# The softmax maxima of a cross-attention kernel are split and turned on VectorE

## The chip, the cores and the metric

The kernel runs on one core of one Trainium2 chip. The metric is device time in microseconds (us), the median of the runs; lower is better. The core has TensorE (PE, its weight loads are listed as PEld), VectorE (DVE), ScalarE (ACT), GpSimd (POOL) and the queues that issue DMAs (SP among them). They run beside each other, each in the order of its own program, and wait for each other by semaphores.

## The reference

Cross-attention with pre-norm on both inputs, 32 batches of 512 tokens, width 512, 16 heads of 32:

```python
B, N_q, _ = q.shape                       # 32, 512, 512; kv has the same shape
qn  = layer_norm(q,  q_norm_g,  q_norm_b)
kvn = layer_norm(kv, kv_norm_g, kv_norm_b)
Q = (qn @ Wq), K = (kvn @ Wk), V = (kvn @ Wv)      # each cut into 16 heads of 32
scores = einsum('bhqd,bhkd->bhqk', Q, K) / sqrt(32)
attn = softmax(scores, axis=-1)
ctx  = einsum('bhqk,bhkd->bhqd', attn, V)
out  = q + gelu(ctx @ Wo + bo, approximate=False)
```

All of it is float32. The softmax needs, for each query and head, a shift by the largest score of its row.

## The kernel before

**Tiling.** A batch is worked off in four steps (s = 0 to 3). A step takes one unit: four heads (128 columns of Q and K). What stands in a step belongs to several units and batches at once: the scores `s` (queries in the partitions, only for the maxima) of the unit one ahead, the scores `st` (keys in the partitions), exponentials and products `pv` with V of the unit itself, the projections `q` and `k` of the unit two ahead, the row sums `z` of the unit behind; and over the batch the projections `v`, the output projections `o` (of the batch before) and the transposes `x` of the tokens (of the batch after).

**The order is written out by hand.** `ORDER` (from line 51) lists for each engine and step the kinds in the order in which the engine takes them; `s*4` is four times `s`. PE takes a projection (12 matmuls of 512 columns) in six parts of two, woven between the scores. An engine never overtakes itself.

**How the maxima get into the scores.** In a step DVE reduces 16 `s` tiles, each to 128 negated maxima (L706), one column of `maxes` each: column 4n+c holds the maxima of head n for the c-th chunk of 128 queries. The shift is then added by TensorE itself: of the 128 rows that `st` contracts, rows 96 to 127 hold the maxima (`q_stack`) against a mask of heads (`k_stack`). For this the maxima have to lie in 32 rows, queries along the free axis, and as a high part rounded to the matmul's input format (16 rows) and the rest (16 rows), so that nothing of them is lost. That goes over five instructions:

1. `md`, DVE L765: copies the 16 columns beside themselves (a maximum over groups of one).
2. `m`, PE L965: one 128x128 transpose of `maxes` into a PSUM bank of the `gen` ring.
3. `mh`, ACT L613: rounds (and for the low rows negates) 32x128 into `max_cut`.
4. `ml`, DVE L771: adds for the low rows the unrounded value, into `max_hl`.
5. `mx`, ACT L617, four times: writes 32x512 of `q_stack`, masked by chunk (a column of `chunk_mask`). The first `st` of the next step waits for all four (`shift_rows`).

**PSUM.** Four banks hold scores (a bank is free when its exponential, L563, or maximum, L706, has been taken), one holds `ctx`, and three (`gen0` to `gen2`) go round among everything in `GEN`: q, k, v, o, x, z and m. Which bank comes next, and whose release it waits for, follows from the order on PE alone.

**Output side.** The output projection of a chunk is followed on DVE by `ob` (L747, adds the bias in the bank), on ACT by `gelu` (L580, into `act_out`, with a table load before the first and one before the next exponential, L563), and on POOL by `res_add`. Of the four chunks of a batch, the `ob` and `gelu` of the third stand at the end of step 1, around `md`, `mh` and `mx`; the fourth stands in step 2.

Of the kernel before, what the change touches and what calls it, by code (L numbers as in the profile page):

```python
# [12 lines left out]
P = 128  # L13
# [47 lines left out]
    ),  # L61
    "act": (
# [4 lines left out]
    ),  # L67
    "dve": (
# [93 lines left out]
for _s in range(NU):  # L162
    for _kind, _n, _part in PLAN["pe"][_s]:
# [3 lines left out]
        if _part == 0 and _kind in ("q", "k", "m", "z"):  # L167
            _off = _s + {"q": 2, "k": 2, "m": 1, "z": -1}[_kind]
            GEN_AT[(_kind, _off % NU)] = len(GEN)
            GEN.append((_kind, _off // NU, _off % NU, NU))  # L170
# [8 lines left out]
def build(nc, x, ctx_in, q_g, q_b, kv_g, kv_b, wq, wk, wv, wo, bo, out):  # L179
    B = x.shape[0]  # L180
    with ExitStack() as es:
# [6 lines left out]
        def sem(name):  # L188
            return es.enter_context(nc.semaphore(name))
# [19 lines left out]
        maxes = sb("maxes", [P, 2, P])  # L209
        max_cut = sb("max_cut", [P, P], F32R)  # L210
        max_hl = sb("max_hl", [P, P], F32R)
        cut_sign = sb("cut_sign", [P, 1])
        low_row = sb("low_row", [P, 1])
# [20 lines left out]
        full = {k: sem(f"{k}_in_psum") for k in "vomzxqk"}  # L234
        free = {k: sem(f"{k}_out_of_psum") for k in "vomzxqk"}
# [8 lines left out]
        max_cut_done = sem("max_cut_done")  # L244
        max_copied = sem("max_copied")
# [191 lines left out]
        def _(pool):  # L437
# [3 lines left out]
            pool.memset(low_row[:], 0.0).then_inc(consts, 1)  # L441
            pool.memset(cut_sign[:], 1.0).then_inc(consts, 1)
            pool.memset(act_out[:], 0.0).then_inc(act_out_free, 1)
            pool.wait_ge(consts, 5)
            pool.affine_select(out=ident[:], in_=ident[:], compare_op=ALU.not_equal, fill=1.0, base=0,
                               pattern=[[-1, P]], channel_multiplier=1).then_inc(consts, 1)
            pool.wait_ge(consts, 6)
            pool.affine_select(out=cut_sign[:], in_=cut_sign[:], compare_op=ALU.is_ge, fill=-1.0,
                               base=SROW + SHIFTS // 2 - 1, pattern=[[0, 1]], channel_multiplier=-1).then_inc(consts, 1)
            pool.wait_ge(consts, 7)  # L450
            pool.affine_select(out=low_row[:], in_=low_row[:], compare_op=ALU.is_ge, fill=1.0,
                               base=SROW + SHIFTS // 2 - 1, pattern=[[0, 1]], channel_multiplier=-1).then_inc(consts, 1)
# [56 lines left out]
        def _(act):  # L509
# [36 lines left out]
            def batch(b):  # L546
                PLAN = plan_of(b)
                for s in range(NU):
# [4 lines left out]
                    for kind, n, part in PLAN["act"][s]:  # L553
# [71 lines left out]
        def _(dve):  # L625
            dve.memset(maxes[:], 0.0)
# [64 lines left out]
            def batch(b):  # L691
                PLAN = plan_of(b)
                for s in range(NU):
# [298 lines left out]
```

## Time and profile before

| | |
|---|---|
| median of 3 runs | 3264.93 us (3263.69 to 3266.2) |
| the profiled execution | 3262.8 us, of it 3261.0 us from first to last instruction |
| PE busy | 3230.8 us (99%), 16611 matmuls |
| DVE, ACT, POOL busy | 2256.9 us (69%), 2280.3 us (70%), 2313.9 us (71%) |
| TensorE's granted clock | 0.998 of full speed |
| one batch | about 99.7 us, nearly the same for batches 1 to 30 |

Matmuls overlap in the profile (a matmul of 512 columns is listed with 0.39 to 0.41 us, and the next one starts 0.23 us after it), so what a PE instruction costs is read from the starts of its neighbours. In a timeline the columns are: start in us, length in us, engine, line, operation, tiles, shapes, count; in brackets the idle time of the engine before it and what ended it. A row of several instructions (x4) gives the time from the first start to the last end.

### The profile page before, as it was taken

To read this page: it belongs to the slowest core of one execution; us is meant where nothing else is said; L and a number is where in the kernel's file an instruction comes from. 1 tells how busy PE (TensorE), PEld (TensorE's weight loads), DVE (VectorE), ACT (ScalarE), POOL (GpSimd) and SP (SyncE) were. 2 spreads that over 40 slices of the span, in tenths; PEclk is the share of its full clock that TensorE was granted. 3 is DMA by queue.
4 is the path that set the end of the run, shared out by engine and by line. 5 is a ranking of instruction groups with operands and counts; after the bars stand their busy time and mean duration, and the time that the engine had idled before them with its cause. 6 is when DMAs were issued, how large, how long until landed. Compare 5 with 4: busy or idle time off the path is not lost.

```text
span 3261.0 us, 49855 instructions
## 1 busy us (share of the span) xinstructions
PE 3230.8 (99%) x16611; PEld 2135.1 (65%) x16611; DVE 2256.9 (69%) x4769; ACT 2280.3 (70%) x3985; POOL 2313.9 (71%) x1544
## 2 busy tenths in 40 slices
PE   8999999999999999999999999999999999999998
PEld 5566666666666666666666666666666666666664
DVE  6667667676676676666766766766667767667664
ACT  5677666777767777667767667776777676677765
POOL 3676776777677767777776677777767776777765
PEclk9999999999999999999999999999999999999999
DMA  5655656566556656565665566665656655666653
GB/s 142 87 108 107 108 104 116 91 111 107 107 104 104 111 107 107 104 118 89 111 109 106 105 102 111 109 104 104 120 86 112 107 107 107 100 111 108 105 79 76
DMA packets 186721, 343.02 MB, mean 105 GB/s; under 512 B 20561, under 2 KB 20577, under 8 KB 186466
## 3 DMA queue, kind: packets, MB, share of 16 engines
q1 hardware_dynamic: 186000, 339.03, 60.0%
q8 instruction: 134, 2.20, 0.3%
q10 hardware_dynamic: 466, 0.80, 0.2%
q14 instruction: 121, 0.99, 0.1%
HBM read 104.87 MB, written 33.55 MB: 42 GB/s over the span
## 4 chain that ended last, share of the span: by engine, by line
PE 97%; DVE 1%; ACT 1%; issue 1%; DMA 0%; POOL 0%; SPq 0%; ACTq 0%; POOLq 0%; DVEq 0%
PE gen L856 43%; PE score L883 16%; PE score L876 15%; PE ctx L903 14%; PE gen L847 4%; PE gen L943 4%; PE gen L965 1%; DVE maxes L706 1%; DMA k_stack<-k_nat 0%; ACT q_stack L617 0%; PE score L788 0%; ACT probs L563 0%; DVE stats L725 0%; PE gen L837 0%; POOL probs L475 0%
## 5 line engine op out<-in xcount | busy, mean ns | idle before, releaser
L475 POOL TENSOR_TENSOR probs<-probs 128x1024 f32<-128x1024 f32 x762 | 1800.3, 2392 | 287.8 <-PE ctx L903 281.6
L706 DVE TENSOR_REDUCE maxes<-score 128x1 f32<-128x512 f32 x2048 | 1294.9, 680 | 217.5 <-PE score L883 213.9
L563 ACT ACTIVATE probs<-score 128x512 f32<-128x512 f32 x2048 | 1090.2, 621 | 141.1 <-PE score L876 137.5
L883 PE MATMUL score<-k_stack,q_stack 96*128 96x512 f32 x2048 | 761.2, 413 | 3.3 <-DVE maxes L706 1.8
L876 PE MATMUL score<-q_stack,k_stack 128*128 128x512 f32 x2048 | 696.4, 406 | 6.6 <-ACT q_stack L617 6.5
L883 PEld LDWEIGHTS score<-k_stack,q_stack 96*128 96x128 f32 x2048 | 378.2, 188 | 221.3 <-ACT probs L563 83.6
L876 PEld LDWEIGHTS score<-q_stack,k_stack 128*128 128x128 f32 x2048 | 374.7, 188 | 199.9 <-DVE maxes L706 64.4
L903 PE MATMUL ctx<-probs,v_sb 128*32 128x512 f32 x4096 | 492.5, 598 | 0.0
L856 PE MATMUL gen<-cT,w_k 128*128 128x512 f32 x1536 | 461.7, 400 | 0.2 <-DVE q_nat L688 0.2
L856 PE MATMUL gen<-w_v,cT 128*128 128x512 f32 x1536 | 461.4, 395 | 0.0
L856 PE MATMUL gen<-xT,w_q 128*128 128x512 f32 x1536 | 447.9, 394 | 0.0
L856 PE MATMUL gen<-w_o,ctx_hl 128*128 128x512 f32 x1488 | 416.4, 396 | 0.0
L491 POOL TENSOR_TENSOR rstd<-var_eps,minus_half 128x1 f32<-128x1 f32 x256 | 140.5, 549 | 335.0 <-DVE neg_mean L737 333.1
L502 POOL TENSOR_TENSOR ctx_hl<-ctx_n,ctx_hl 128x512 fp32r<-128x512 f32 x128 | 164.2, 1283 | 290.4 <-ACT ctx_hl L569 290.4
L617 ACT ACTIVATE q_stack<-max_hl,chunk_mask 32x512 fp32r<-32x512 f32 x512 | 326.3, 706 | 42.3 <-DVE max_hl L771 41.5
L856 PEld LDWEIGHTS gen<-w_v,cT 128*128 128x128 f32 x1536 | 287.3, 189 | 84.1 <-issue 26.8
L856 PEld LDWEIGHTS gen<-xT,w_q 128*128 128x128 f32 x1536 | 288.5, 190 | 60.6
L856 PEld LDWEIGHTS gen<-cT,w_k 128*128 128x128 f32 x1536 | 287.5, 192 | 55.2 <-DVE q_nat L688 1.1
L688 DVE SCALAR_TENSOR_TENSOR k_nat<-gen,bias_k,k_nat 128x512 fp32r<-128x512 f32 x128 | 95.8, 748 | 318.0 <-ACT k_nat L608 318.0
L856 PEld LDWEIGHTS gen<-w_o,ctx_hl 128*128 128x128 f32 x1488 | 276.7, 189 | 57.3
L903 PEld LDWEIGHTS ctx<-probs,v_sb 128*32 128x32 f32 x4096 | 106.9, 109 | 233.8 <-issue 233.8
L574 ACT ACTIVATE v_sb<-gen 128x512 f32<-128x512 f32 x128 | 76.5, 598 | 255.1 <-PE gen L856 255.1
(89 smaller groups left out, 2765.4 us busy)
## 6 DMA issues: line engine op xcount, KB each, us to landing
k_stack<-k_nat SPq DMA_DIRECT2D x384, 256.0 KB, 7.6
q_stack<-q_nat SPq DMA_DIRECT2D x381, 256.0 KB, 5.6
tok<-in_x SPq DMA_DIRECT2D x132, 256.0 KB, 11.0
tok<-in_ctx SPq DMA_DIRECT2D x128, 256.0 KB, 12.0
res<-in_x SPq DMA_DIRECT2D x124, 256.0 KB, 2.7
out<-res SPq DMA_DIRECT2D x124, 256.0 KB, 2.1
probs<-in_L_xattn_Wq SPq DMA_DIRECT2D x1, 1024.0 KB, 8.2
probs<-in_L_xattn_Wk SPq DMA_DIRECT2D x1, 1024.0 KB, 10.4
```

What stands on the lines that cost most here:

```text
L475: pool.tensor_tensor(probs[:, c + 1, heads], probs[:, c + 1, heads], probs[:, c, heads], ALU.add).then_inc(pool_added, 1)
L491: pool.tensor_tensor(rstd[:, n:n + 1], var_eps[:, n:n + 1], minus_half[:], ALU.pow).then_inc(ln_rstd, 1)
L502: pool.tensor_tensor(ctx_hl[:, 1, up], ctx_n[:], raw(ctx_hl[:, 0, up]), ALU.subtract).then_inc(ctx_split, 1)
L563: act.activation(probs[:, n, part, :], score_at(s, "st", i)[:], ACT.Exp, scale=SCALE).then_inc(exp_done, 1)
L617: act.activation(q_stack[SROW:P, u1 % 2, :, P * n:P * (n + 1)], raw(max_hl[SROW:P, :]).unsqueeze(1).to_broadcast([SHIFTS, HU, P]), ACT.Ide ...
L706: dve.tensor_reduce(maxes[:, u1 % 2, SROW + i:SROW + i + 1], score_at(s, "s", i)[:], AX_X, ALU.max, negate=True).then_inc(max_done, 1)
L847: mm = pe.matmul(bank[DH * j:DH * (j + 1), :], ones[:, 0:DH], probs[:, c, j, :], start=(i == 0), stop=(i == len(chunks) - 1))
L856: mm = pe.matmul(bank[:, :], stationary(hs, c), moving(hm, c), start=(i == 0), stop=(i == len(TERMS) * NC - 1))
L876: pe.matmul(score_bank(pe, b, s, "st", i)[:, :], k_stack[:, s % 2, part, P * n:P * (n + 1)], q_stack[:, s % 2, part, :], start=True, stop= ...
L883: pe.matmul(score_bank(pe, b, s, "s", i)[:, :], q_stack[0:KROWS, u1 % 2, n, P * part:P * (part + 1)], k_stack[0:KROWS, u1 % 2, n, :], star ...
L903: mm = pe.matmul(ctx_ps[DH * j:DH * (j + 1), :], v_sb[:, c, lo:lo + DH], probs[:, c, j, :], start=(c == 0), stop=(c == NC - 1))
L943: mm = pe.matmul(bank[:, P * c:P * (c + 1)], tok[:, n, P * c:P * (c + 1)], ident[:], start=True, stop=True, is_transpose=True)
```

## The change

The transpose on PE and the rounding on ACT go; DVE does both. `md` keeps its place in DVE's order and now stands for six instructions:

- a reduction over groups of one writes the 16 columns rounded into `max_split[:, 0:16]`;
- `scalar_tensor_tensor` writes `maxes * 1 - rounded` into `max_split[:, 16:32]`; it waits for the first by a semaphore;
- four `transpose` of 32x32 turn partitions 32g to 32g+31 of `max_split` into rows 96 to 127 of `max_hl`, columns 32g to 32g+31; the first waits for the subtraction.

`mh`, `m` and `ml` leave the orders, which otherwise stay as they are; `mx` waits for the four transposes. `m` also leaves the ring of `gen` banks. Two memsets and two selects at the start of the program go.

```diff
@@ ORDER
     "pe": (
-        "st s k s*2 pv m k o*2 k o k*2",
+        "st s k s*2 pv k o*2 k o k*2",
...
     "act": (
...
-        "st*6 gelu q st x st*2 norm st*4 x k st*2 norm x norm st x*2 norm x norm x*2 gelu mh gelu mx*4 split",
+        "st*6 gelu q st x st*2 norm st*4 x k st*2 norm x norm st x*2 norm x norm x*2 gelu gelu mx*4 split",
...
     "dve": (
...
-        "ln la*2 q zt lv*2 x la zr ln zb cn lv s la x k lv s x s*2 x*2 s*2 x s*3 x s*2 x s ob s*4 md ob ml",
-        "s ob s*6 zt s zr zb cn s k s*7 md q ml",
+        "ln la*2 q zt lv*2 x la zr ln zb cn lv s la x k lv s x s*2 x*2 s*2 x s*3 x s*2 x s ob s*4 md ob",
+        "s ob s*6 zt s zr zb cn s k s*7 md q",
@@ GEN
-        if _part == 0 and _kind in ("q", "k", "m", "z"):
+        if _part == 0 and _kind in ("q", "k", "z"):
@@ scalar engine
-                        if kind == "mh" and valid(b1):
-                            wait(act, full["m"], NU * b1 + u1 + 1)
-                            wait(act, free["m"], NU * b1 + u1)
-                            act.activation(max_cut[SROW:P, :], gen_at("m", u1)[SROW:P, 0:P], ACT.Identity,
-                                           scale=cut_sign[SROW:P, 0:1]).then_inc(max_cut_done, 1)
                         if kind == "mx" and valid(b1):
-                            wait(act, free["m"], NU * b1 + u1 + 1)
+                            wait(act, max_turned, HU * (NU * b1 + u1 + 1))
@@ vector engine
                         if kind == "md" and valid(b1):
                             wait(dve, max_done, 16 * (t1 + 1))
-                            dve.tensor_reduce(maxes[:, u1 % 2, SROW + SHIFTS // 2:P],
-                                              maxes[:, u1 % 2, SROW:SROW + SHIFTS // 2].unsqueeze(2), AX_X,
-                                              ALU.max).then_inc(max_copied, 1)
-                        if kind == "ml" and valid(b1):
-                            wait(dve, max_cut_done, t1 + 1)
+                            dve.tensor_reduce(max_split[:, 0:SHIFTS // 2], maxes[:].unsqueeze(2), AX_X,
+                                              ALU.max).then_inc(max_high, 1)
+                            wait(dve, max_high, t1 + 1)
+                            dve.scalar_tensor_tensor(out=max_split[:, SHIFTS // 2:SHIFTS], in0=maxes[:], scalar=ones[:, 0:1],
+                                                     in1=raw(max_split[:, 0:SHIFTS // 2]), op0=ALU.mult,
+                                                     op1=ALU.subtract).then_inc(max_low, 1)
                             wait(dve, shift_rows, NC * t1)
-                            dve.scalar_tensor_tensor(out=max_hl[SROW:P, :], in0=gen_at("m", u1)[SROW:P, 0:P],
-                                                     scalar=low_row[SROW:P, 0:1], in1=raw(max_cut[SROW:P, :]),
-                                                     op0=ALU.mult, op1=ALU.add).then_inc(free["m"], 1)
+                            wait(dve, max_low, t1 + 1)
+                            for g in range(P // SHIFTS):
+                                rows = slice(SHIFTS * g, SHIFTS * (g + 1))
+                                dve.transpose(max_hl[SROW:P, rows], raw(max_split[rows, :])).then_inc(max_turned, 1)
@@ tensor engine
-                        if kind == "m" and valid(b1):
-                            bank = gen_bank(pe, b, "m", u1)
-                            wait(pe, max_copied, t1 + 1)
-                            pe.matmul(bank[:, 0:P],
-                                      maxes[:, u1 % 2, :], ident[:], start=True, stop=True,
-                                      is_transpose=True).then_inc(full["m"], 1)
```

How the rows of the program stand, in a batch in the middle. DVE at the end of step 1, before: L706 is the maximum of a score tile, L765 `md`, L747 `ob`, L771 `ml`.

```order
L706 TENSOR_REDUCE maxes<-score3 128x1 [waits s_full]
L765 TENSOR_REDUCE maxes<-maxes 128x16 [waits max_done]
L747 TENSOR_TENSOR gen1<-gen1,bias_all 128x512 [waits o_in_psum]
L771 SCALAR_TENSOR_TENSOR max_hl<-gen0,low_row,max_cut 32x128 [waits shift_rows,max_cut_done]
L706 TENSOR_REDUCE maxes<-score0 128x1 [waits s_full,m_in_psum]
L747 TENSOR_TENSOR gen2<-gen2,bias_all 128x512 [waits o_in_psum]
```

The same place in the changed kernel: L689 is the maximum of a score tile, L730 `ob`.

```order
L689 TENSOR_REDUCE maxes<-score3 128x1 [waits s_full]
L748 TENSOR_REDUCE max_split<-maxes 128x16 [waits max_done]
L751 SCALAR_TENSOR_TENSOR max_split<-maxes,ones,max_split 128x16 [waits max_high]
L758 STREAM_TRANSPOSE max_hl<-max_split 32x32 [waits max_low,shift_rows]
L758 STREAM_TRANSPOSE max_hl<-max_split 32x32 x3
L730 TENSOR_TENSOR gen0<-gen0,bias_all 128x512 [waits o_in_psum]
L689 TENSOR_REDUCE maxes<-score0 128x1 [waits s_full]
```

Before, one instruction stood between the last maximum and `ob`; now six do.

ACT at the same place, before and then after: L580 and L571 are `gelu`, L617 and L603 `mx`, L569 and L560 the split of `ctx`, L563 and L554 the exponentials.

```order
L580 ACTIVATE act_out<-gen2 128x512 [waits o_biased]
L613 ACTIVATE max_cut<-gen0,cut_sign 32x128 [waits m_out_of_psum,m_in_psum]
L580 ACTIVATE act_out<-gen1 128x512 [waits act_out_free,o_biased]
L617 ACTIVATE q_stack<-max_hl,chunk_mask 32x4x128 [waits m_out_of_psum] x4
L569 ACTIVATE ctx_hl<-ctx_n 128x512 [waits o_in_psum,ctx_read]
L580 ACTIVATE act_out<-gen2 128x512 [waits act_out_free,o_biased]
L563 ACT_TABLE_LOAD [waits st_full]
L563 ACTIVATE probs<-score0 128x512 [waits pool_added]
```

```order
L571 ACTIVATE act_out<-gen1 128x512 [waits o_biased]
L571 ACTIVATE act_out<-gen0 128x512 [waits act_out_free,o_biased]
L603 ACTIVATE q_stack<-max_hl,chunk_mask 32x4x128 [waits max_turned] x4
L560 ACTIVATE ctx_hl<-ctx_n 128x512 [waits o_in_psum,ctx_read]
L571 ACTIVATE act_out<-gen1 128x512 [waits act_out_free,o_biased]
L554 ACT_TABLE_LOAD [waits st_full]
L554 ACTIVATE probs<-score0 128x512 [waits pool_added]
```

The rounding is gone from between the two gelus; the second gelu still stands ahead of `mx` and still waits for its `ob`.

PE at the end of step 2, before and then after: L903 and L888 are `pv`, L965 is `m`, L856 and L841 are projections.

```order
L903 MATMUL ctx<-probs,v_sb 32x512 x7
L965 MATMUL gen1<-ident,maxes 128x128 [waits max_copied,k_out_of_psum]
L856 MATMUL gen2<-cT,w_k 128x512 [waits z_out_of_psum]
L856 MATMUL gen2<-cT,w_k 128x512
L856 MATMUL gen0<-xT,w_q 128x512 [waits q_out_of_psum]
L856 MATMUL gen0<-xT,w_q 128x512
L856 MATMUL gen2<-cT,w_k 128x512 x2
L856 MATMUL gen1<-w_v,cT 128x512 [waits x_out_of_psum,m_out_of_psum]
```

```order
L888 MATMUL ctx<-probs,v_sb 32x512 x7
L841 MATMUL gen2<-cT,w_k 128x512 [waits k_out_of_psum]
L841 MATMUL gen2<-cT,w_k 128x512
L841 MATMUL gen0<-xT,w_q 128x512 [waits z_out_of_psum]
L841 MATMUL gen0<-xT,w_q 128x512
L841 MATMUL gen2<-cT,w_k 128x512 x2
L841 MATMUL gen1<-w_v,cT 128x512 [waits x_out_of_psum,q_out_of_psum]
```

The transpose is gone, and the first matmul of `v` waits for the bank of the `q` of the step before (released by DVE's L673, the L688 of before) where it waited for the bank of `m`.

## Rows read from the trace of the kernel before

**Rows 1.** The page: busy times, and the chain that ended last.
```profile
PE 3230.8 (99%) x16611; PEld 2135.1 (65%) x16611; DVE 2256.9 (69%) x4769; ACT 2280.3 (70%) x3985; POOL 2313.9 (71%) x1544
PE 97%; DVE 1%; ACT 1%; issue 1%; DMA 0%; POOL 0%; SPq 0%; ACTq 0%; POOLq 0%; DVEq 0%
```

**Rows 2.** Timeline of PE, seam of steps 1 and 2.
```profile
1011.90 0.30 PE L965 MATMUL gen<-ident,maxes 128*128 128x128 f32 x1
1011.95 2.07 PE L856 MATMUL gen<-w_o,ctx_hl 128*128 128x512 f32 x8
1013.86 0.40 PE L883 MATMUL score<-k_stack,q_stack 96*128 96x512 f32 x1
...
1016.20 0.40 PE L876 MATMUL score<-q_stack,k_stack 128*128 128x512 f32 x1
```

**Rows 3.** Timeline of PE, a `pv` without and one with `m` behind.
```profile
1027.20 0.73 PE L883 MATMUL score<-k_stack,q_stack 96*128 96x512 f32 x2
1027.76 0.40 PE L856 MATMUL gen<-xT,w_q 128*128 128x512 f32 x1
...
1032.75 0.33 PE L965 MATMUL gen<-ident,maxes 128*128 128x128 f32 x1
1032.83 0.71 PE L856 MATMUL gen<-cT,w_k 128*128 128x512 f32 x2
1033.38 0.62 PE L856 MATMUL gen<-xT,w_q 128*128 128x512 f32 x2
```

**Rows 4.** Timeline of DVE, seam of steps 1 and 2.
```profile
1009.07 2.47 DVE L706 TENSOR_REDUCE maxes<-score 128x1 f32<-128x512 f32 x4
1011.58 0.17 DVE L765 TENSOR_REDUCE maxes<-maxes 128x16 f32<-128x16 f32 x1
1011.67 0.69 DVE L747 TENSOR_TENSOR gen<-gen,bias_all 128x512 f32<-128x512 f32 x1
1012.63 0.36 DVE L771 SCALAR_TENSOR_TENSOR max_hl<-gen,low_row,max_cut 32x128 fp32r<-32x128 f32 x1 [0.27 <-ACT max_cut L613]
```

**Rows 5.** Timeline of ACT, the same seam.
```profile
1012.24 0.36 ACT L613 ACTIVATE max_cut<-gen,cut_sign 32x128 fp32r<-32x128 f32 x1 [2.44 <-PE gen L965]
1012.62 0.60 ACT L580 ACTIVATE act_out<-gen 128x512 f32<-128x512 f32 x1
1013.24 2.55 ACT L617 ACTIVATE q_stack<-max_hl,chunk_mask 32x512 fp32r<-32x512 f32 x4
...
1016.35 0.58 ACT L580 ACTIVATE act_out<-gen 128x512 f32<-128x512 f32 x1
1016.95 1.28 ACT L563 ACT_TABLE_LOAD   x1
1018.25 2.06 ACT L563 ACTIVATE probs<-score 128x512 f32<-128x512 f32 x4
```

**Rows 6.** Timeline of PE's weight loads, step 2 and the start of step 3.
```profile
1018.90 0.19 PEld L883 LDWEIGHTS score<-k_stack,q_stack 96*128 96x128 f32 x1 [0.26 <-ACT probs L563]
...
1034.07 0.41 PEld L856 LDWEIGHTS gen<-w_v,cT 128*128 128x128 f32 x2
...
1036.51 0.30 PEld L876 LDWEIGHTS score<-q_stack,k_stack 128*128 128x128 f32 x2 [0.21 <-ACT q_stack L617]
```

**Rows 7.** Groups of instructions on DVE (count | busy us, mean ns | idle before).
```profile
L688 DVE SCALAR_TENSOR_TENSOR q_nat<-gen,bias_q,q_nat 128x512 fp32r<-128x512 f32 x128 | 95.5, 746 | 222.5 <-ACT q_nat L594 222.5
L711 DVE STREAM_TRANSPOSE ctx_n<-gen 128x512 f32<-128x512 f32 x128 | 90.3, 705 | 62.4 <-PE gen L847 62.4
```

**Rows 8.** Timeline of DVE, seams of steps 2 and 3, and of 0 and 1.
```profile
1032.04 0.17 DVE L765 TENSOR_REDUCE maxes<-maxes 128x16 f32<-128x16 f32 x1
...
1078.80 0.17 DVE L765 TENSOR_REDUCE maxes<-maxes 128x16 f32<-128x16 f32 x1
1080.20 0.36 DVE L771 SCALAR_TENSOR_TENSOR max_hl<-gen,low_row,max_cut 32x128 fp32r<-32x128 f32 x1 [1.23 <-ACT max_cut L613]
1080.59 0.69 DVE L725 BATCH_NORM_STATS2 stats<-tok 128x6 f32<-128x512 f32 x1
```

More of the change, by code:

```diff
@@ L53 @@
         "q*3 v q*2 v q v st*2 v*2 s st v s st s v*2 st s st s z v st*3 s v*2 st*2 s st k v s*4 pv st s st*2 o s "
[1 row of a table removed]
[1 row of a table added]
         "o st*2 o st*3 q st q*4 st q st*3 z x k*3 x st*2 x st k*2 s k st s st*2 pv s x s x s x s pv s x s*2 o*3 "
[1 row of a table removed]
[1 row of a table added]
         "o*4 s o s k s k s st k s st z st s st s q st q st s st*2 k st*3 k s st k st*4 pv s*2 q s q s*2 q s*2 q "
[1 row of a table removed]
[1 row of a table added]
         "k q k v q v k*2 st*3 k st*2 q st*2 k q st q st q st*2 z st*4 v st v s*3 pv s*2 v s*2 v s*2 v s v s*2 v*2 "
[1 row of a table removed]
[1 row of a table added]
     ),
     "act": (
[4 rows of a table removed]
+        "q st*4 v st*8 norm v split norm*2 st*4 mx*4 k",
+        "st*6 gelu q st x st*2 norm st*4 x k st*2 norm x norm st x*2 norm x norm x*2 gelu gelu mx*4 split",
+        "gelu st*12 k split st*4 q mx*4",
+        "st*6 k st*5 q st*4 split st v*2 mx*4",
     ),
     "dve": (
[4 rows of a table removed]
[4 rows of a table added]
     ),
@@ L208, in build @@
         ones = sb("ones", [P, P])
[L209 to L213, printed above, removed]
+        maxes = sb("maxes", [P, SHIFTS // 2])
+        max_split = sb("max_split", [P, SHIFTS], F32R)
+        max_hl = sb("max_hl", [P, P])
         chunk_mask = sb("chunk_mask", [P, NC])
@@ L232, in build @@
         gen = [ps(f"gen{i}") for i in range(NGEN)]
-        full = {k: sem(f"{k}_in_psum") for k in "vomzxqk"}
-        free = {k: sem(f"{k}_out_of_psum") for k in "vomzxqk"}
+        full = {k: sem(f"{k}_in_psum") for k in "vozxqk"}
+        free = {k: sem(f"{k}_out_of_psum") for k in "vozxqk"}
         st_full = sem("st_full")
@@ L243, in build @@
         x_hi = sem("x_hi")
-        max_cut_done = sem("max_cut_done")
-        max_copied = sem("max_copied")
+        max_high = sem("max_high")
+        max_low = sem("max_low")
+        max_turned = sem("max_turned")
         shift_rows = sem("shift_rows")
@@ L440, in _ @@
             pool.memset(minus_half[:], -0.5).then_inc(consts, 1)
-            pool.memset(low_row[:], 0.0).then_inc(consts, 1)
-            pool.memset(cut_sign[:], 1.0).then_inc(consts, 1)
             pool.memset(act_out[:], 0.0).then_inc(act_out_free, 1)
-            pool.wait_ge(consts, 5)
+            pool.wait_ge(consts, 3)
             pool.affine_select(out=ident[:], in_=ident[:], compare_op=ALU.not_equal, fill=1.0, base=0,
                                pattern=[[-1, P]], channel_multiplier=1).then_inc(consts, 1)
[L447 to L452, printed above, removed]
             def prepare(b, s):
@@ L702, in batch @@
                             i = NC * n + part
-                            if i == 0:
-                                wait(dve, full["m"], t1 - 1)
                             wait(dve, s_full, 16 * t1 + i + 1)
-                            dve.tensor_reduce(maxes[:, u1 % 2, SROW + i:SROW + i + 1], score_at(s, "s", i)[:], AX_X, ALU.max,
+                            dve.tensor_reduce(maxes[:, i:i + 1], score_at(s, "s", i)[:], AX_X, ALU.max,
                                               negate=True).then_inc(max_done, 1)
@@ L886, in batch @@
                             wait(pe, ctx_split, NU * B - 2)
-                            for kind2, count in (("z", NU * B - 1), ("m", NU * B), ("q", NU * B), ("k", NU * B),
+                            for kind2, count in (("z", NU * B - 1), ("q", NU * B), ("k", NU * B),
                                                  ("x", 2 * NC * B), ("v", NC * B), ("o", NC * (B - 1))):
```

9 lines of the change are left out of this document (4 added, 5 removed), and 13 rows, old and new, of the table ORDER.

## The prediction

> **What bounds the kernel now.** I read the page first. PE is busy for 99% of the span and the chain that ended last runs through PE for 97% of it [rows 1]; all other engines stand at 69 to 71%. That says that PE work taken away is worth its time, if nothing else becomes late. It doesn't say that nothing else can: a share is an average, and the chain of waits only names an engine where another one stood still for it. So I then read the timelines of PE, DVE, ACT and the weight loads at the four places where `m` stands, which I call seams: 1-2 (1011.9 us), 2-3 (1032.8), 3-0 and 0-1. The batches in the middle repeat each other within a few hundredths of a us, so one batch does for all.
>
> Two things are to be seen there. First, `m` is cheap for PE. Second, at seam 1-2 there is a tight train of work on ACT: the rounding (1012.24), the gelu of the third chunk (1012.62), four `mx` (1013.24 to 1015.79), the split, the gelu of the fourth chunk, a table load, the first exponential (1018.25), each starting within 0.03 us of the end of the one before or sooner [rows 5]. PE loads weights for a score at 1018.90, after a wait of 0.26 us that the end of that first exponential (1018.25 + 0.60) ends [rows 6]. What delays the train delays PE one for one.
>
> **What PE gets back.** Without `m`, two matmuls behind a `pv` take 1027.76 - 1027.20 = 0.56 us. With it, from `m` at 1032.75 to the third matmul behind it at 1033.38 are 0.63 us [rows 3]. So `m` costs 0.07 us at the three seams behind a `pv`. At seam 1-2 it takes 0.05 us itself, and the eight matmuls behind it need 1.91 us where eight at 0.23 us need 1.84: 0.12 us [rows 2]. The weights of `m` lie beside other work in all of them. Added up, PE has 0.33 us less per batch.
>
> **The first `st` behind `mx`.** At seams 2-3 and 0-1 its weight load waits 0.21 us for `q_stack` [rows 6], and as the load then doesn't run ahead of the matmul, it costs some 0.05 us. If `mx` comes earlier, this goes.
>
> **What DVE gets instead.** Before: `md`, 0.17 us, and `ml`, 0.36 us [rows 4], with idle time in between. After: six instructions in a row.
> - The reduction: 0.17 us, as `md`; it starts 0.04 us behind the last maximum (1009.07 + 2.47 = 1011.54, then 1011.58), because it waits for that result [rows 4]. The next two waits on a result get the same 0.04.
> - The subtraction, 128x16: not in the trace in this size. The same kind of operation takes 0.746 us for 512 columns [rows 7] and 0.36 for 128 [rows 4], so 1.0 ns per column and 0.25 us for 16. Bounds: 0.17 (`md`) to 0.36.
> - Four transposes of 32x32: not in the trace. The transpose of 512 columns takes 0.705 us [rows 7]; 480 columns less, at 1.0 to 1.04 ns, leave 0.21 to 0.22. What matters more is how closely they follow each other. `ob` starts 0.09 us after `md`, before the latter has ended [rows 4]. But behind `ml`, which works on partitions 96 to 127, the next instruction starts 0.03 us after its end (1080.20 + 0.36, then 1080.59), though it waits for nothing of it [rows 8]. The four transposes read four different groups of 32 partitions and write the last group; they are nearer to that row. I take 0.21 + 0.03 = 0.24 us for each. Bounds: 0.09 (they overlap as `md` and `ob` do) to 0.39 (as `ml` and its follower).
>
> The Trainium skill ("VectorE: DVE Perf Modes", section "Two Vector instructions with no wait between them") has a rule for this: an instruction whose input or output starts in another group of 32 partitions than the last one in that memory is held until all earlier ones have finished. The trace agrees, with 0.03 us behind `ml` against an overlap of 0.08 behind `md`. By the rule all four transposes are held, and the instruction behind them; a sum without the rule is the second rival below.
>
> Together, from the end of the last maximum: 0.04 + 0.17 + 0.04 + 0.25 + 0.04 + 4 x 0.24 = 1.50 us. Four such blocks are 6 us of a batch of 100 on an engine that is busy for 69% [rows 1]: DVE is no bound in its sum. So it depends on what is queued behind the block.
>
> **Seam 1-2.** Behind the block stands the `ob` of the third chunk, and on ACT the gelu that waits for it stands ahead of `mx`. Before, `ob` ran at 1011.67 to 1012.36, well inside ACT's wait for the rounding. After: it starts at 1011.54 + 1.50 = 1013.04, ends 0.69 later at 1013.73, and the gelu starts at 1013.76 instead of 1012.62: 1.14 us later. That the rounding is gone from ACT doesn't help, since ACT now waits for DVE. `mx` ends 1.14 us later, at 1016.93, so PE stands before the first `st` (1016.20 before, [rows 2]) for some 0.8 us; then split, gelu, table load and the first exponential come 1.14 later, and the score of 1018.90 goes at 1020.04. The 0.12 us that `m` frees here only make the wait longer. Net: +1.14 us in each batch that has an `ob` in step 1 and steady neighbours, 30 of them: +34 us. Bounds: with 0.17 and 0.09, the gelu comes 0.46 later (+14 us); with 0.36 and 0.39, 1.85 later (+55 us).
>
> **Seam 2-3.** The block ends at 1032.04 - 0.04 + 1.50 = 1033.50 [rows 8], `mx` can start there, earlier than it did; the 0.05 us wait of `st` goes. But the low part of q (L688) now stands behind the block: 1033.50 + 0.75 = 1034.25. It releases the bank that the first `v` takes, since `m` has left the ring. Its weight load stood at 1034.07 [rows 6] and would now be due 0.07 earlier; it waits until about 1034.29, and matmul and load then start together. New wait: 0.17 us against the old time, less 0.12 for the shortened step from load to matmul and what is lost behind it, plus 0.05. I take +0.10 and -0.05: +0.05, times 31: +1.6 us. Low bound -0.12 (no wait), high bound +0.7 (with the long transposes).
>
> **Seams 3-0 and 0-1.** Nothing that is due stands behind the block; the maxima are ready no later than with `ml`. -0.07 and -0.07 - 0.05, times 31: -5.9 us. At the head and the end of the program the new block is as long as the old way over PE and ACT: nothing.
>
> **Sum:** 34.2 + 1.6 - 5.9 = +29.9 us, to 3292.7 us for the profiled execution (3262.8). The median of the timed runs lies 2.1 us above the profiled one, at 3264.93; from it, 3294.8 us. I say 3294.
>
> **Rivals.**
> 1. *The maxima are simply cheaper, and the kernel gets faster.* For it: PE is the bound [rows 1], loses 128 instructions, and DVE and ACT have 30% to spare. If the train of seam 1-2 is no later than before, all of PE's terms count: (0.33 + 2 x 0.05) x 31 = 13 us less, 3252. Against it: the train has no slack [rows 5], and `ob` would have to start by 1011.90, with six instructions ahead of it. It decides at a delay of the third gelu of 0.25 us: below it the kernel gets faster, above it slower.
> 2. *No hold between the transposes.* They follow each other at 0.21 - 0.08 = 0.13 us. The block is 1.06 us, the gelu 0.70 later (+21), no wait for q's bank (-0.12 x 31 = -3.7), -5.9: +11 to +14, about 3278. For it: nearly all pairs on DVE overlap; against it: the row behind `ml`.
> 3. *Short small instructions*, near the lower bounds: +14 - 3.7 - 5.9 = +4, about 3270. Against it: nothing on DVE with this many columns is that short when it waits.
> 4. *Long transposes*, the upper bounds: +55 + 21 - 5.9 = +70, 3335. For it: a transpose has to take in a block before it gives one out; against it: for 512 columns it takes hardly longer than other operations.
>
> **Chances.** Main case 0.66; no hold 0.17; short 0.06; long 0.05; faster 0.06. The range takes in the second rival and most of the third: 3270 to 3306. The measurement can tell 0.2%, 6.5 us, from no change; the third rival is about half below it, and some of the second may come near: faster 0.06, same 0.08, slower 0.86.
>
> **What would show it.** In the profile after: transposes of about 0.21 us, starting 0.24 apart; between the last maximum and `ob` at the end of step 1 about 1.5 us; on ACT a gelu of the third chunk that waits for DVE's `ob` and starts 2.2 us after the last maximum has ended, where it was 1.1; on PE's weight loads a wait of 0.8 us or more for `q_stack` at the first `st` of step 2, once a batch (30 times), and a longer wait for the first exponential. At the other seams no wait for `q_stack`, and a small one for q's low part at seam 2-3. A batch takes 1.0 us longer, nearly all of it in the first third of step 2. I am wrong if `ob` and gelu start less than 0.4 us later than before, or if PE makes the time up elsewhere in the batch, which its 99% leave no room for.

## The result and the profile after

The changed kernel takes 3519.47 us (median, 3517.19 to 3526.04), the kernel before 3264.31 beside it: ratio 1.0784, 95% interval 1.0765 to 1.0803. It is slower, as forecast, but by 255 us where I had 30, and far outside the range (3270 to 3306). The profiled execution spans 3524.2 us.

The page of the changed kernel, busy times (against [rows 1]) and the chain that ended last, by engine and by line:

```profile
span 3524.2 us, 49594 instructions
PE 3308.1 (94%) x16483; PEld 2166.2 (61%) x16483; DVE 2545.4 (72%) x5280; ACT 2238.4 (64%) x3857; POOL 2309.5 (66%) x1540
PE 40%; DVE 36%; ACT 17%; issue 6%; DMA 0%; DVEq 0%; ACTq 0%
```

PE went from 97% of the chain to 40%, and DVE from 1% to 36%, while DVE is busy for only 72%. DVE's busy time rose by 288.5 us. One group of instructions holds most of that (count | busy us, mean ns | idle before), against [rows 7]:

```profile
L751 DVE SCALAR_TENSOR_TENSOR max_split<-maxes,ones,max_split 128x16 fp32r<-128x16 f32 x128 | 217.9, 1702 | 4.5
```

The new instructions, by tile (minimum, median and maximum in ns):

```profile
L758 DVE STREAM_TRANSPOSE max_hl<-max_split x512: 204/204/210, 58.9 to 3489.9; 32x32 f32<-32x32 f32 x171
L748 DVE TENSOR_REDUCE max_split<-maxes x128: 169/170/172, 58.5 to 3486.6; 128x16 fp32r<-128x16 f32 x128
L751 DVE SCALAR_TENSOR_TENSOR max_split<-maxes,ones,max_split x128: 234/2022/4496, 58.7 to 3486.8; 128x16 fp32r<-128x16 f32 x128
```

The reduction (0.17 us) and the transposes (0.20) are what the prediction said. The subtraction of 16 columns is not: 0.234 us at its shortest, 2.022 in the median, 4.496 at its longest. The seam of steps 1 and 2 on DVE, the answer to [rows 4]:

```profile
1192.89 0.17 DVE L748 TENSOR_REDUCE max_split<-maxes 128x16 fp32r<-128x16 f32 x1
1193.10 2.18 DVE L751 SCALAR_TENSOR_TENSOR max_split<-maxes,ones,max_split 128x16 fp32r<-128x16 f32 x1
1195.39 0.91 DVE L758 STREAM_TRANSPOSE max_hl<-max_split 32x32 f32<-32x32 f32 x4
1196.33 0.70 DVE L730 TENSOR_TENSOR gen<-gen,bias_all 128x512 f32<-128x512 f32 x1
...
1216.70 2.29 DVE L751 SCALAR_TENSOR_TENSOR max_split<-maxes,ones,max_split 128x16 fp32r<-128x16 f32 x1
1219.10 0.91 DVE L758 STREAM_TRANSPOSE max_hl<-max_split 32x32 f32<-32x32 f32 x4
1220.05 0.75 DVE L673 SCALAR_TENSOR_TENSOR q_nat<-gen,bias_q,q_nat 128x512 fp32r<-128x512 f32 x1
...
3459.87 4.50 DVE L751 SCALAR_TENSOR_TENSOR max_split<-maxes,ones,max_split 128x16 fp32r<-128x16 f32 x1
```

What GpSimd does at the same three places (L466 adds the exponentials of two chunks, SBUF to SBUF, L490 adds the residual):

```profile
1192.83 2.42 POOL L466 TENSOR_TENSOR probs<-probs 128x1024 f32<-128x1024 f32 x1
...
1216.59 2.38 POOL L466 TENSOR_TENSOR probs<-probs 128x1024 f32<-128x1024 f32 x1
...
3453.64 7.10 POOL L466 TENSOR_TENSOR probs<-probs 128x1024 f32<-128x1024 f32 x3
3460.71 1.29 POOL L490 TENSOR_TENSOR res<-res,act_out 128x512 f32<-128x512 f32 x1
3461.96 2.37 POOL L466 TENSOR_TENSOR probs<-probs 128x1024 f32<-128x1024 f32 x1
```

The first subtraction ends at 1193.10 + 2.18 = 1195.28, and GpSimd's add at 1192.83 + 2.42 = 1195.25. The second: 1218.99 and 1218.97. The longest ends at 3464.37, 0.04 us after the last of the three GpSimd instructions that it ran beside (3464.33). A VectorE instruction that ends a few hundredths of a us after a GpSimd instruction, whatever its own size, is what a wait inside an instruction looks like: no semaphore holds it, and the profile counts the time as busy. Over the whole trace it is so for 127 of the 128 subtractions: each ends 0.03 to 0.04 us behind a GpSimd instruction. The one that is left ran beside none and took 0.234 us. By place, the subtraction takes 2.14 us in the median at the seam of steps 1 and 2, 2.30 at 2-3, 1.98 at 3-0, and only 0.37 at 0-1, where the GpSimd instruction beside it was about to end.

ACT at the seam of steps 1 and 2, against [rows 5], and then PE:

```profile
1197.07 0.60 ACT L571 ACTIVATE act_out<-gen 128x512 f32<-128x512 f32 x1 [5.96 <-DVE gen L730]
1197.69 2.54 ACT L603 ACTIVATE q_stack<-max_hl,chunk_mask 32x512 fp32r<-32x512 f32 x4
```

```profile
1200.28 0.50 PE L861 MATMUL score<-q_stack,k_stack 128*128 128x512 f32 x1 [2.69 <-ACT q_stack L603]
...
1220.86 0.73 PE L841 MATMUL gen<-w_v,cT 128*128 128x512 f32 x2 [1.99 <-DVE q_nat L673]
```

The gelu of the third chunk, `mx`, and the first `st` follow each other as reckoned, 2 us later than reckoned. The wait for q's bank at the seam of steps 2 and 3, forecast at 0.17 us, is 1.99. The same in the waits of the whole run (us, times, longest):

```profile
ACT q_stack L603 <- DVE max_hl L758: 370.0, 97, 8.2
ACT act_out L571 <- DVE gen L730: 223.1, 62, 8.7
PE score L861 <- ACT q_stack L603: 128.0, 66, 6.1
PE gen L841 <- DVE q_nat L673: 62.1, 31, 2.0
```

Last, the clock. The mean granted clock is 0.976, against 0.998 before. Five stretches of the changed kernel (busy us and instructions of PE, PEld, DVE, ACT and POOL, then the granted clock):

```profile
1300.00:1326.00 26.00, 23.32 (x111) 14.19 (x109) 18.87 (x30) 15.72 (x27) 13.34 (x8) 0.93 0.37 82
1326.00:1334.00 8.00, 5.99 (x19) 4.66 (x19) 1.91 (x6) 3.88 (x7) 7.30 (x4) 0.79 0.64 92
1192.00:1200.00 8.00, 5.59 (x25) 4.23 (x23) 7.67 (x14) 2.91 (x5) 4.52 (x3) 1.00 0.22 71
1200.30:1204.00 3.70, 3.50 (x17) 1.67 (x18) 0.83 (x2) 3.67 (x6) 2.51 (x2) 1.00 0.10 34
1306.60:1310.30 3.70, 3.70 (x14) 1.50 (x15) 0.69 (x1) 3.41 (x5) 2.51 (x2) 0.67 0.08 28
```

The second has part of its time at the lower level (1.2 instead of 2.4 GHz), behind an idle time of PE of 2.01 us that ended at 1328.19. In the third PE stood idle for 2.69 us, until 1200.28, and the fourth, right behind it, lies at full clock. The fifth stands at the same place of the next batch, right behind an idle time of 2.68 us, and has part of its time at the lower level. The matmuls in the second stretch are some 0.43 us apart instead of 0.23:

```profile
1328.19 1.14 PE L841 MATMUL gen<-w_v,cT 128*128 128x512 f32 x2 [2.01 <-DVE q_nat L673]
1329.13 1.06 PE L841 MATMUL gen<-xT,w_q 128*128 128x512 f32 x2
1329.98 1.06 PE L841 MATMUL gen<-w_v,cT 128*128 128x512 f32 x2
```

In all, some 172 us of the run lie at the lower level, against 15 before.

### The profile page after: what moved, and what is told of

The parts are those of the page before. It is cut to its first block, busy times and chain, and to the rows that moved or that the text cites. A ratio compares the mean times of both kernels' runs of the same rounds, so it can differ in the third digit from the quotient of the medians.

```text
span 3524.2 us, 49594 instructions
## 1 busy us (share of the span) xinstructions
PE 3308.1 (94%) x16483; PEld 2166.2 (61%) x16483; DVE 2545.4 (72%) x5280; ACT 2238.4 (64%) x3857; POOL 2309.5 (66%) x1540
## 4 chain that ended last, share of the span: by engine, by line
PE 40%; DVE 36%; ACT 17%; issue 6%; DMA 0%; DVEq 0%; ACTq 0%
DVE maxes L689 21%; PE gen L841 14%; PE score L861 11%; DVE max_split L751 6%; PE score L868 6%; ACT probs L554 6%; ACT q_stack L603 6%; PE ctx L888 5%; DVE max_hl L758 3%; PE gen L832 3%; DVE cT L671 2%; ACT L554 1%; ACT xT L579 1%; DVE gen L730 1%; DVE xT L671 1%
## 5 line engine op out<-in xcount | busy, mean ns | idle before, releaser
L466 POOL TENSOR_TENSOR probs<-probs 128x1024 f32<-128x1024 f32 x762 | 1795.7, 2386 | 391.2 <-PE ctx L888 383.3
L689 DVE TENSOR_REDUCE maxes<-score 128x1 f32<-128x512 f32 x2048 | 1300.8, 683 | 246.8 <-PE score L868 240.6
L554 ACT ACTIVATE probs<-score 128x512 f32<-128x512 f32 x2048 | 1094.7, 620 | 208.2 <-PE score L861 205.9
L861 PE MATMUL score<-q_stack,k_stack 128*128 128x512 f32 x2048 | 712.8, 414 | 128.0 <-ACT q_stack L603 128.0
L861 PEld LDWEIGHTS score<-q_stack,k_stack 128*128 128x128 f32 x2048 | 383.7, 192 | 350.8 <-ACT q_stack L603 156.3
L603 ACT ACTIVATE q_stack<-max_hl,chunk_mask 32x512 fp32r<-32x512 f32 x512 | 325.9, 705 | 370.8 <-DVE max_hl L758 370.0
L841 PE MATMUL gen<-w_v,cT 128*128 128x512 f32 x1536 | 479.6, 408 | 62.1 <-DVE q_nat L673 62.1
L888 PE MATMUL ctx<-probs,v_sb 128*32 128x512 f32 x4096 | 492.5, 598 | 0.0
L841 PE MATMUL gen<-cT,w_k 128*128 128x512 f32 x1536 | 474.9, 409 | 0.1
L841 PE MATMUL gen<-xT,w_q 128*128 128x512 f32 x1536 | 458.8, 401 | 0.7 <-ACT v_sb L565 0.7
L841 PE MATMUL gen<-w_o,ctx_hl 128*128 128x512 f32 x1488 | 410.7, 394 | 0.0
L841 PEld LDWEIGHTS gen<-w_v,cT 128*128 128x128 f32 x1536 | 291.0, 193 | 161.8 <-DVE q_nat L673 75.4
L841 PEld LDWEIGHTS gen<-cT,w_k 128*128 128x128 f32 x1536 | 294.3, 197 | 112.1 <-issue 52.8
L841 PEld LDWEIGHTS gen<-xT,w_q 128*128 128x128 f32 x1536 | 294.9, 194 | 91.6 <-issue 26.0
L673 DVE SCALAR_TENSOR_TENSOR k_nat<-gen,bias_k,k_nat 128x512 fp32r<-128x512 f32 x128 | 95.9, 749 | 340.5 <-ACT k_nat L599 340.5
L841 PEld LDWEIGHTS gen<-w_o,ctx_hl 128*128 128x128 f32 x1488 | 278.3, 189 | 59.2
L673 DVE SCALAR_TENSOR_TENSOR q_nat<-gen,bias_q,q_nat 128x512 fp32r<-128x512 f32 x128 | 95.8, 749 | 217.6 <-ACT q_nat L585 216.6
L888 PEld LDWEIGHTS ctx<-probs,v_sb 128*32 128x32 f32 x4096 | 106.9, 109 | 235.6 <-issue 235.6
```

The source lines that it names most:

```text
L466: pool.tensor_tensor(probs[:, c + 1, heads], probs[:, c + 1, heads], probs[:, c, heads], ALU.add).then_inc(pool_added, 1)
L554: act.activation(probs[:, n, part, :], score_at(s, "st", i)[:], ACT.Exp, scale=SCALE).then_inc(exp_done, 1)
L673: dve.scalar_tensor_tensor(out=dst, in0=psum, scalar=bias, in1=raw(hi), op0=ALU.add, op1=ALU.subtract).then_inc(done, 1)
L689: dve.tensor_reduce(maxes[:, i:i + 1], score_at(s, "s", i)[:], AX_X, ALU.max, negate=True).then_inc(max_done, 1)
L841: mm = pe.matmul(bank[:, :], stationary(hs, c), moving(hm, c), start=(i == 0), stop=(i == len(TERMS) * NC - 1))
L861: pe.matmul(score_bank(pe, b, s, "st", i)[:, :], k_stack[:, s % 2, part, P * n:P * (n + 1)], q_stack[:, s % 2, part, :], start=True, stop= ...
```

## The experiments

The theory after the result: an instruction of VectorE with two inputs in SBUF waits until the GpSimd instruction that runs beside it has ended. Rivals: the subtraction is slow by itself; the rounded output makes it slow; the placement of the block is what costs.

**e1: the same place, the same tile, no second input.** The subtraction becomes a reduction over groups of one of the rounded half.

```diff
-dve.scalar_tensor_tensor(out=max_split[:, 16:32], in0=maxes[:], scalar=ones[:, 0:1],
-                         in1=raw(max_split[:, 0:16]), op0=ALU.mult, op1=ALU.subtract)
+dve.tensor_reduce(max_split[:, 16:32], raw(max_split[:, 0:16]).unsqueeze(2), AX_X, ALU.max)
```

> The subtraction (two tensors from SBUF) is replaced by a reduction over groups of one that reads the rounded half and writes the other half of max_split: the same place, the same dependences, one input. The low part of the maxima is then wrong. Theory P (the subtraction waits for GpSimd's running instruction, because it reads two tensors from SBUF): the instruction takes 0.17 us, the block 1.4 us, and the time is what the recorded prediction had summed up without the wait, 3264 + 28 = 3292 us (3280 to 3300). Rival D (the wait comes from reading and writing one tile, or from the semaphore in front of it): it still takes 2 us and the time stays at 3519 us.

Measured: 3293.14 us (3292.42 to 3293.79), ratio 1.0088 [1.0071, 1.0105]; beside it before 3264.61. One seam of steps 1 and 2 on DVE, then ACT and the weight loads:

```profile
1118.34 1.27 DVE L689 TENSOR_REDUCE maxes<-score 128x1 f32<-128x512 f32 x2
1119.65 0.17 DVE L748 TENSOR_REDUCE max_split<-maxes 128x16 fp32r<-128x16 f32 x1
1119.85 0.17 DVE L751 TENSOR_REDUCE max_split<-max_split 128x16 fp32r<-128x16 f32 x1
1120.13 0.92 DVE L757 STREAM_TRANSPOSE max_hl<-max_split 32x32 f32<-32x32 f32 x4
1121.07 0.70 DVE L730 TENSOR_TENSOR gen<-gen,bias_all 128x512 f32<-128x512 f32 x1
```

```profile
1121.81 0.60 ACT L571 ACTIVATE act_out<-gen 128x512 f32<-128x512 f32 x1 [3.94 <-DVE gen L730]
1122.43 2.55 ACT L603 ACTIVATE q_stack<-max_hl,chunk_mask 32x512 fp32r<-32x512 f32 x4
```

```profile
1125.03 0.19 PEld L860 LDWEIGHTS score<-q_stack,k_stack 128*128 128x128 f32 x1 [1.12 <-ACT q_stack L603]
...
1128.08 0.19 PEld L867 LDWEIGHTS score<-k_stack,q_stack 96*128 96x128 f32 x1 [0.50 <-ACT probs L554]
```

226 of the 255 us go with one input. The block is 1.46 us long, and the gelu starts 2.20 us after the last maximum. The recorded working, with 0.17 instead of 0.25 us for this instruction, gives 1.42 and 2.14. And this reduction lies wholly within the time of one GpSimd add in 127 of its 128 places, and still takes 0.17 us.

**e2: the second input stays, GpSimd is short.** Its adds L466 take 8 columns of each head instead of 512.

```diff
-pool.tensor_tensor(probs[:, c + 1, heads], probs[:, c + 1, heads], probs[:, c, heads], ALU.add)
+pool.tensor_tensor(probs[:, c + 1, heads, 0:8], probs[:, c + 1, heads, 0:8], probs[:, c, heads, 0:8], ALU.add)
```

> The changed kernel, but GpSimd's sums of exponentials (six a step, 128x1024, 2.4 us each) take 8 columns per head instead of 512 (128x16): the row sums miss most of their terms. The subtraction stays as it is. Theory P: the subtraction takes 0.24 us except where the residual's or the split's 1.3 us instruction runs; 3275 to 3300 us. Rival D: 2 us, 3519 us less at most a little.

Measured: 3298.29 us, ratio 1.0103 [1.0083, 1.0123]. The unchanged subtraction, by tile, and the adds:

```profile
L751 DVE SCALAR_TENSOR_TENSOR max_split<-maxes,ones,max_split x128: 233/235/299, 61.0 to 3261.8; 128x16 fp32r<-128x16 f32 x128
```

```profile
L466 POOL TENSOR_TENSOR probs<-probs 128x16 f32<-128x16 f32 x762 | 155.0, 221 | 1094.1 <-PE ctx L888 1080.7 <-issue 6.7 <-ACT probs L554 4.8
```

The instruction's own length is 0.235 us (mean 0.252), as predicted from the 128-column and 512-column rows. It isn't slow by itself, and its rounded output doesn't make it slow. GpSimd's length sets it.

**e3: one SBUF input, but another operation.**

```diff
+dve.tensor_scalar(max_split[:, 16:32], raw(max_split[:, 0:16]), 1.0, None, ALU.mult)
```

> In the place of the subtraction a tensor_scalar (times 1) of the rounded half, 128x16, one input from SBUF; the low part of the maxima is wrong. If only two input tensors make an instruction wait for GpSimd: 0.15 us, 3285 to 3295 us. If an operation with one input that VectorE can run at two elements a cycle waits too, which is the wide form of theory P: about 2 us, 3500 to 3520 us.

Measured: 3519.74 us (3513.71 to 3525.77), ratio 1.0781, and this by tile:

```profile
L751 DVE TENSOR_SCALAR max_split<-max_split x128: 175/2023/4492, 58.7 to 3486.5; 128x16 fp32r<-128x16 f32 x128
```

The theory in its narrow form falls: this instruction has one input in SBUF and waits like the subtraction. The reduction of e1, with the same input and output, does not. So it isn't the count of inputs alone; the kind of operation matters. Its size matters too: the kernel before has 512 `tensor_scalar` of one column, from SBUF to SBUF (L736 and L737), 94 of them wholly within the time of a GpSimd instruction, and none takes over 0.154 us:

```profile
L736 DVE TENSOR_SCALAR var_eps<-moments x256: 94/140/154, 6.4 to 3092.5; 128x1 f32<-128x1 f32 x128
```

The Trainium skill ("SBUF — State Buffer", sections "Who interferes with whom" and "Summary: rules for kernel authors") has both cases: a VectorE instruction with two SBUF inputs, beside a GpSimd instruction that reads SBUF, or one in a 2-port mode, goes for an interface that it shares with GpSimd, and the second one to issue "**fully blocks** until the first finishes". The traces of after and e2 agree for two inputs (2.022 against 0.235 us in the median), and e3 fits the other case (2.023), though a trace doesn't show an instruction's mode. "Until the first finishes" is less than was measured: the subtraction of 4.50 us above waited over two instructions that GpSimd began later than it did.

**e8: the kernel before, with one such instruction added.** It stands behind `md`, nothing waits for it, and its output isn't used.

```diff
 dve.tensor_reduce(maxes[:, u1 % 2, 112:128], ...).then_inc(max_copied, 1)
+dve.scalar_tensor_tensor(out=spare_low[:], in0=maxes[:, u1 % 2, 96:112], scalar=ones[:, 0:1],
+                         in1=z_inv[:], op0=ALU.mult, op1=ALU.subtract)
```

> The kernel before, whole, with one instruction more: behind md a scalar_tensor_tensor of 128x16 of two SBUF tensors (maxes and z_inv) into a spare tile that nobody reads, with no semaphore. PE's transpose, ACT's rounding and ml stay. Theory P: it takes 0.3 to 2.3 us by what GpSimd is running, and what stands behind it on DVE (ob, ml, q's low part) comes so much later: 3264 + 100 to 230 us, say 3420. Rival D (the wait belonged to the new chain of instructions on max_split): 0.24 us each, hidden in the idle time before ml: 3264 to 3272 us.

Measured: 3427.56 us, ratio 1.0503 [1.0484, 1.0522], 164 us for 128 instructions of 16 columns:

```profile
L769 DVE SCALAR_TENSOR_TENSOR spare_low<-maxes,ones,z_inv x128: 226/2119/4625, 59.5 to 3391.1; 128x16 f32<-128x16 f32 x128
```

Again 126 of the 128 end 0.03 to 0.04 us behind a GpSimd instruction. The wait needs nothing of the change but this kind of instruction at this place. The longest are twice what I had as the most (2.3 us).

**e4: the whole computation without the wait.** The reduction of e1 is run a second time with the sign turned, so that the rounded value with a minus lies beside each maximum, and a third reduction adds the pairs.

```diff
+dve.tensor_reduce(max_split[:, 0:16], maxes[:, :, 0:1], AX_X, ALU.max)
+dve.tensor_reduce(maxes[:, :, 1].bitcast(F32R), maxes[:, :, 0:1], AX_X, ALU.max, negate=True)
+dve.tensor_reduce(max_split[:, 16:32], maxes[:], AX_X, ALU.add)
```

> The whole computation with no instruction of two SBUF tensors: maxes gets a second column per maximum, which a reduction fills with minus the rounded maximum, and the rest is a reduction with add over the pair. One instruction more than the changed kernel. Theory P: no wait; the block is 0.1 us longer than that of the one-input experiment, 3295 us (3283 to 3305). Rival D: 3519 us or more.

Measured: 3298.77 us, ratio 1.0105 [1.0089, 1.012]. The reduction of pairs takes 0.186 us. This is what the change costs once the wait is away.

**e6 and e5: e4 with `ob`, or with `ob` and the low part of q, ahead of the block.**

```diff
-"... s ob s*4 md ob",
+"... s ob s*4 ob md",
-"s ob s*6 zt s zr zb cn s k s*7 md q",
+"s ob s*6 zt s zr zb cn s k s*7 q md",    # e5 alone
```

> The three-reduction kernel with the ob of the third chunk put ahead of md in step 1 (an edit of DVE's order alone). Theory S (without the wait for GpSimd, the cost is the ob and the gelu behind the block at seam 1-2): the gelu starts at its old place, mx 0.35 us later than in the kernel before instead of 1.2 later: 3298.8 - 30 x 0.8 = 3274 us (3268 to 3280). Rival Q (the cost lies in DVE's longer block wherever it stands, and in q's low part): 3290 to 3299 us.

> As the one with ob first, and the low part of q put ahead of md in step 2 too. The v of step 3 no longer waits for q's bank (0.05 to 0.1 us a batch back), but the block ends 0.65 us later, mx with it, and the first st of step 3 waits some 0.25 us: slower than ob first alone by 3 to 8 us, 3279 us. If q's bank was the larger cost: faster by 3 us or more.

Measured: e6 3280.57 us, ratio 1.0052 [1.0039, 1.0066], so 18 us of the 34 come back, not 24, and the time lies just outside what I expected (3268 to 3280); e5 3282.35, ratio 1.0058 [1.0042, 1.0073]. The two intervals overlap, so moving q as well brings nothing that can be told; I had expected it to cost 3 to 8 us. The seam of steps 1 and 2 is the larger part of the loss, as reckoned, but with `ob` first `mx` becomes late in its turn (PE's weight loads wait 27.1 us in all for `q_stack` in e6, 40.5 in e5).

**e7: the changed kernel with the order of e5.**

> The changed kernel with its subtraction of two SBUF tensors, ob and q's low part put ahead of md. Theory P says that the wait for GpSimd stands inside the chain from the last maximum to mx, so the order behind it saves only v's wait for q's bank (62 + 75 us of waiting on PE's side, overlapping) and the gelu's 0.6 us: 3440 to 3490 us. If the cost was mainly what is queued behind the block: 3300 to 3340 us.

Measured: 3451.43 us (3446.65 to 3456.22), ratio 1.0568 [1.053, 1.0605]. Placement gives 68 us of the 255, as expected (3440 to 3490). Putting these two ahead doesn't take the wait away: the subtraction's mean is still 1.594 us, and `mx`, which needs it, is still late:

```profile
PE score L861 <- ACT q_stack L603: 157.2, 97, 6.1
```

**e9: the changed kernel with all four transposes reading partitions 0 to 31.**

```diff
-dve.transpose(max_hl[SROW:P, rows], raw(max_split[rows, :]))
+dve.transpose(max_hl[SROW:P, rows], raw(max_split[0:SHIFTS, :]))
```

> The changed kernel, but all four transposes read partitions 0 to 31 (the maxima of three quarters of the queries are then those of the first quarter). If an instruction is held because it reads another group of 32 partitions than the last one: the second to fourth start 0.12 to 0.13 us apart instead of 0.235. If they are held for another reason (the small size, the transposing itself): 0.235 us as before. The time: 3519 us less at most 15.

Measured, one run: 3451.34 us. At a seam of steps 1 and 2:

```profile
1167.21 2.17 DVE L751 SCALAR_TENSOR_TENSOR max_split<-maxes,ones,max_split 128x16 fp32r<-128x16 f32 x1
1169.49 0.48 DVE L758 STREAM_TRANSPOSE max_hl<-max_split 32x32 f32<-32x32 f32 x4
1169.90 0.66 DVE L730 TENSOR_TENSOR gen<-gen,bias_all 128x512 f32<-128x512 f32 x1
```

Four transposes take 0.48 us here and 0.91 in the changed kernel. They start 0.09 us apart (expected: 0.12 to 0.13) instead of 0.236, and each is shorter:

```profile
L758 DVE STREAM_TRANSPOSE max_hl<-max_split x512: 161/163/206, 60.5 to 3414.7; 32x32 f32<-32x32 f32 x171
```

What holds them is that each reads another group of 32 partitions than the one before; the output group is the same in both kernels. On the time my expectation was a miss: 68 us went where I had at most 15. PE's long gaps (starts over 0.56 us apart, counted beyond 0.23) add up to 262 us in the changed kernel and 210 here, so 52 us less of standing still, some 0.55 us at each of three seams in 31 batches, where the transposes by themselves save 0.43. I had counted the saving at one seam. Some of the rest may be the clock: 119 us of this run lie at the lower level, against 172. No experiment separates it.

**e10: the old way at two seams, the new one at the other two.** At the seams of steps 1-2 and 2-3 the block delays something, so there the transpose on PE and the rounding on ACT stay. At 3-0 and 0-1 nothing due stands behind it, so there DVE does both, with the reductions of e4.

```diff
-"... pv m k o*2 ..."   (step 0)     +"... pv k o*2 ..."
-"s*2 v s*2 v pv m",    (step 3)     +"s*2 v s*2 v pv",
 # m, mh and ml stay in steps 1 and 2; in steps 3 and 0 md stands for:
+def turn_on_dve(b1, u1, t1):
+    # three tensor_reduce as in e4, then
+    for g in range(P // SHIFTS):
+        dve.transpose(max_hl[SROW:P, rows], raw(max_split[rows, :])).then_inc(max_turned, 1)
```

> The way over PE and ACT stays at seams 1-2 and 2-3, where something is queued behind the maxima on DVE; at seams 3-0 and 0-1 the maxima are split by three reductions and turned on DVE. By the terms of the recorded sum (0.07 and 0.12 us a batch): 3264.6 - 6 = 3258.6 us (3256 to 3262). If PE's slots don't come back as time, or a block of 1.5 us is in the way at these seams too: 3264 to 3275 us.

Measured: 3258.41 us (3257.38 to 3259.22, 11 runs), ratio 0.9983 [0.9974, 0.9992]. It beats both kernels, the one before by 0.17%: 5.2 us, below the 0.2% that I called the limit, but the 95% interval of the ratio leaves out 1. PE has 9.1 us less to do (3221.7 busy against 3230.8), and 5 to 6 of them reach the end.

## Why the prediction was wrong

- **The step that failed** is the second bullet of "What DVE gets instead": the subtraction at 0.25 us, with bounds of 0.17 and 0.36. It measured 1.702 us in the mean. Its own length was right (0.235 us with GpSimd short, e2); the wait inside it was missing, and with it my upper bound was no bound. Shown by e1 and e2 from two sides, and by e8 on the kernel before.
- **Why the trace of before didn't show it.** The rows that I priced from, L688 in [rows 7] and L771 in [rows 4], have an input in PSUM (`gen`). The steady batches have no instruction with both inputs in SBUF; the head and the end of the program have 20, at 512 columns (0.67 to 0.74 us each), which I didn't look at. Four of them would have warned me: the weights' subtractions L641 ran beside a GpSimd instruction, and that one (L464) took 4.97 us, where the same operation at the same size takes 2.2 just before (rows in the last section). I took it for "the same kind of operation" by its name and columns, not by where its inputs lie, and didn't look at what GpSimd, busy for 71% [rows 1], was doing at the block's place. A bound for the unknown would have been one GpSimd instruction longer, some 2.4 us; even that is less than the longest wait here.
- **The rest of the recorded working held.** With the subtraction at 0.17 us, as in e1, the block is 0.08 us shorter at both seams where it delays something, and the same sum gives 29.9 - 0.08 x 30 - 0.08 x 31, or some 25 us; e1 measured 28.5. Point by point in e1, with what the working gives at 0.17 us: block 1.46 us (1.42), gelu 2.20 us after the last maximum (2.14), a wait of 1.12 us of the weight load for `q_stack` (0.8 or more), the first exponential's wait 0.50 where it was 0.26 [rows 6], and transposes of 0.205 us, each held until the one before has ended (0.21, 0.03).
- **What a block longer by some 2 us does besides**, which the sum of short waits doesn't contain: the bank of q is late by 2.0 us at each seam 2-3 (62.1 us in all), `mx` is late at 3-0 as well, where I had written that nothing due stands behind, and the clock falls at times. A batch takes 108.9 us in the median, against 99.8 before and 100.8 in e1.
- **The size of the clock's part** was not separated by an experiment. PE's long gaps hold 262 us in the changed kernel and 67 in e1, which is 195 of the 234 us between their spans. Matmuls begun at the lower level take 110 us against 10, and at full speed would take about half, which leaves some 50 us. The two come to 245 us where 234 are to be had: they are estimates, and agree with the whole within 11 us.
- **The rivals.** Both "no hold" and "short small instructions" are refuted by the transposes' 0.24 us pitch, and "long transposes" by the same, with its 0.39. "The kernel gets faster" fails even without the wait (e1, 28.5 us slower), but holds where nothing stands behind the block (e10). The direction and the place (seam of steps 1 and 2 first) were right for the part that I had seen, and that part is a ninth of the whole (28.5 of 255 us).

## What to carry to other kernels

Before pricing a small VectorE instruction by its columns, look where its inputs lie and what GpSimd runs at that moment: here a 16-column instruction with two SBUF inputs cost 2 us and a reduction over the same columns 0.17. If GpSimd is busy for two thirds of the time with long instructions, write such steps as reductions, or read one input from PSUM: in the kernel before, L771, with one input in PSUM and one in SBUF, lies within the time of a GpSimd instruction in 127 of 128 places and never takes over 0.361 us. And taking work off the bounding engine paid here only at the places where nothing due is queued behind the new block, two seams of four.

## What the runs showed of the hardware

- A `tensor_scalar` with one SBUF input waits for GpSimd too if it has 16 columns (175 to 4492 ns, median 2023, e3); with one column it does not (at most 154 ns). A `tensor_reduce` of the same 16 columns never does (169 to 171 ns, e1).
- The waiting instruction can lose more than once: 4.50 us, over the ends of two GpSimd instructions and until that of a third. It ends 0.03 to 0.04 us after GpSimd's.
- GpSimd can be the one that waits. At the head of the kernel before, four instructions with two SBUF inputs keep their own length (0.67 us each), and it is GpSimd's L464 that takes 4.97 us, though it had started 0.55 us before the first of them:

```profile
19.79 2.18 POOL L459 TENSOR_SCALAR v_sb<-probs,norm_cols 128x512 f32<-128x512 f32 x1
21.74 4.97 POOL L464 TENSOR_SCALAR tok<-probs,norm_cols 128x512 f32<-128x512 f32 x1
```

```profile
22.29 2.47 DVE L641 TENSOR_TENSOR w_q<-v_sb,w_q 128x512 fp32r<-128x512 f32 x4
```

In all twelve traces, L464 (or its counterpart) ends 1.93 to 1.96 us behind the last of the four, which is about its own length, whether it started before the first of them (eight traces) or after. So by these rows the recorded starts don't tell which of the two engines waits; what does is open.

- Four 32x32 transposes take 0.91 us if each reads another group of 32 partitions, and 0.48 if all read the same. Their length falls too, from 204 to 163 ns in the median.
- After PE had stood idle for 2.68 us, part of the next 3.7 us lay at the lower level of the clock (granted clock 0.67), and after 2.69 us at the same place of the batch before none of it did (1.00). So the length of the idle time alone doesn't decide it; what does is open.
